# One power instruction for two scales in a macaron block: the order of VectorE's and GpSimd's work in the FFN steps is rewritten

## The reference

```
x = x + 0.5 * ffn(layernorm(x))       # FFN: 128 -> 512 -> 128
x = x + rnn(layernorm(x))             # minGRU, a scan over the 256 tokens of a sequence
x = x + 0.5 * ffn(layernorm(x))       # the same FFN weights again
ffn(v): h = gelu(lin(v, w_up)); return lin(h, w_down)
lin(v, w): v / (rms(v) + 1e-8) @ ternary(w).T,  ternary(w) = sign(w) * (|w| > 0.5 * mean|w|)
layernorm(v): (v - mean) / sqrt(var + 1e-5)
```

## Time and profile before

| what | us |
|---|---|
| median of 3 runs (262.29 to 263.86) | 262.69 |
| the profiled execution's own time | 263.04 |
| its span, first to last instruction | 261.3 |
| mean granted clock of PE, share of full speed | 0.991 |

### The profile page before, as it was taken

How to read it: one execution, slowest core, us unless ns; L and a number is a source line. 1 busy time by engine, 2 the same in 40 slices (tenths; PEclk the granted TensorE clock), 3 DMA queues, 4 the chain that set the end, 5 groups by cost and what they waited for, 6 DMA issues and landing times.

```text
span 261.3 us, 9753 instructions
## 1 busy us (share of the span) xinstructions
PE 236.6 (91%) x3759; PEld 167.1 (64%) x3759; DVE 234.1 (90%) x754; ACT 221.4 (85%) x534; POOL 216.4 (83%) x400
## 2 busy tenths in 40 slices
PE   0759999999998899899999998679999999999992
PEld 0626777777777667655555544357777776777782
DVE  3798799999999998999999999986999999988784
ACT  2377999989998899879999997997899999999861
POOL 5676998989998898599999999998889989997133
PEclk9988999999999999999999999999999999999999
DMA  6990000000000000000000000000111211112114
GB/s 188 300 265 3 4 4 3 3 3 4 3 3 4 3 4 4 3 0 1 3 1 0 0 1 3 3 3 3 43 43 57 67 46 43 43 43 82 46 43 123
DMA packets 18062, 9.73 MB, mean 37 GB/s; under 512 B 608, under 2 KB 17888, under 8 KB 18016
## 3 DMA queue, kind: packets, MB, share of 16 engines
q1 hardware_dynamic: 17744, 8.98, 12.5%
q10 hardware_dynamic: 272, 0.13, 0.2%
HBM read 4.92 MB, written 4.19 MB: 35 GB/s over the span
## 4 chain that ended last, share of the span: by engine, by line
PE 53%; DVE 21%; ACT 7%; POOL 7%; issue 6%; DVEq 0%; ACTq 0%; POOLq 0%
PE Y L502 17%; PE U L458 9%; PE G L489 9%; PE U L459 8%; DVE hidden L701 5%; PE T L439 4%; ACT h_hi L330 4%; DVE st L719 3%; DVE h_lo L654 3%; PE U L518 2%; DVE cand L691 2%; DVE mv L619 2%; PE G L478 2%; POOL xn L236 2%; POOL root L212 2%
## 5 line engine op out<-in xcount | busy, mean ns | idle before, releaser
L654 DVE SCALAR_TENSOR_TENSOR h_lo<-h_hi,U 128x1024 f16<-128x1024 f16 x63 | 75.6, 1215 | 10.0 <-ACT h_hi L330 9.6
L324 ACT ACTIVATE U<-U 128x1024 f32<-128x1024 f32 x63 | 64.7, 1026 | 15.3 <-PE U L459 14.4
L236 POOL TENSOR_SCALAR xn<-X,neg_mean,rstd 128x128 f32<-128x128 f32 x156 | 67.8, 447 | 6.9 <-DVE rstd L624 4.2
L330 ACT ACTIVATE h_hi<-U 128x1024 f16<-128x1024 f32 x63 | 64.7, 1027 | 1.0
L502 PE MATMUL Y<-down_w,h_hi 128*128 128x128 f16 x496 | 59.4, 220 | 0.0
L502 PE MATMUL Y<-down_w_half,h_lo 128*128 128x128 f16 x496 | 59.0, 219 | 0.0
L458 PE MATMUL U<-xt_hi,up_w 128*128 128x512 f16 x128 | 49.2, 384 | 9.4 <-DVE h_lo L654 7.5
L212 POOL TENSOR_TENSOR root<-mv,half 128x8 f32<-128x8 f32 x31 | 51.0, 1644 | 2.3
L459 PE MATMUL U<-xt_lo,up_w 128*128 128x512 f16 x128 | 49.2, 384 | 0.0
L502 PEld LDWEIGHTS Y<-down_w_half,h_lo 128*128 128x128 f16 x496 | 48.5, 98 | 0.4
L502 PEld LDWEIGHTS Y<-down_w,h_hi 128*128 128x128 f16 x496 | 47.7, 98 | 1.6
(11 more groups left out here) (101 smaller groups left out, 415.2 us busy)
## 6 DMA issues: line engine op xcount, KB each, us to landing
X<-in_L_attn_x SPq DMA_DIRECT2D x16, 256.0 KB, 5.3
out_x<-X SPq DMA_DIRECT2D x15, 256.0 KB, 2.8
up_raw<-in_L_ffn_w_up SPq DMA_DIRECT2D x1, 256.0 KB, 4.5
down_raw<-in_L_ffn_w_down SPq DMA_DIRECT2D x1, 256.0 KB, 4.7
out_x<-X SPq DMA_DIRECT2D x1, 128.0 KB, 1.9
out_x<-X ACTq DMA_DIRECT2D x1, 128.0 KB, 2.9
gate_raw<-in_L_attn_Wh SPq DMA_DIRECT2D x1, 64.0 KB, 3.7
gate_raw<-in_L_attn_Wi SPq DMA_DIRECT2D x1, 64.0 KB, 3.6
```

The lines of the kernel that those rows point to most:

```text
L236: m = eng.tensor_scalar(xn[:, n % 2, t, :], X[:, c, :], neg_mean[l][:, c:c + 1], rstd[l][:, c:c + 1], ALU.add, ALU.mult)
L324: eng.activation(U[part][:], U[part][:], ACT.Gelu, scale=1.0 / XN_SPLIT).then_inc(gelu_done, 1)
L330: eng.mul(h_hi[:, F % 2, 2 * part:2 * part + 2, :], U[part][:], H_SPLIT).then_inc(h_hi_done, 1)
L654: vec.scalar_tensor_tensor(out=h_lo[:, F % 2, 2 * part:2 * part + 2, :], in0=h_hi[:, F % 2, 2 * part:2 * part + 2, :], scalar=-1.0 / H_SPL ...
```

## The change

The two powers become one. `ACT` writes the sum of squares of FFN group F into a fourth column of `mv`, beside the variance of the group that is five later in the same layer (`rides_with`, `rider`). POOL then takes one power over 128x4x3 for `ln_roots(l, g)` and adds pairs into a `den` of 128x8, and DVE's `scales` makes both scales in one reciprocal of 128x8. The last five FFN groups of each layer ("alone") keep `rms_step`. The joint power waits for `ssq_done` of F.

Around it the order is rewritten. On POOL `norm` stands first in every step, ahead of the joint power of `ln_roots(k+3)`, and `ln_moments(k+4)` stands last. On DVE in FFN0, `scales(0, k+3)` stands between the two `h_low` of step k, and `stats` and `mean_var` of group k+4 stand behind `add_ffn(k-2)`. The turn into the RNN issues the gates of its first groups one by one on other PSUM banks, and ahead of `gram(15)` and `down(15)`; some RNN steps take five tiles of later statistics instead of four. At the end PE lays `gram(31)` between the tiles of `down(30)`, and the last rows are added and stored in smaller parts.

```
 def ln_roots(l, g):
-    if l == 0 or g >= BY_ACT:
-        ln_moments(l, g)
+    F = rider(l, g)
+    w = 2 if F is None else 3
     pool.wait_ge(var_set[l], 2 * (g if l == 0 else g + 1))
-    eng.tensor_tensor(root[l][:, g % 2], mv[l][:, cols(g), 1:3], half[:], ALU.pow).then_inc(root_done[l], 1)
+    if F is not None:
+        pool.wait_ge(ssq_done, F + 1)
+    eng.tensor_tensor(root[l][:, g % 2, :, 0:w], mv[l][:, cols(g), 1:1 + w], half[:, :, 0:w], ALU.pow).then_inc(root_done[l], 1)
...
 # POOL
-for s in range(0, 3 * groups):
+for s in range(2, 3 * groups):
...
+    if s + 2 < 3 * groups and r != 1:
+        norm(s + 2)
+    if 2 <= k < groups - 3:
+        ln_roots(0, k + 3)
...
+    if 1 <= q < groups - 3:
+        ln_roots(2, q + 3)
...
+    if k + 4 < groups:
+        ln_moments(0, k + 4)
...
+    if 0 <= q < groups - 4:
+        ln_moments(2, q + 4)
...
 # DVE, FFN0
+for k in range(2, groups):
+    if k + 1 < groups:
+        low_part(k + 1)
...
+    h_low(k, 0)
+    if 2 < k < groups - 3:
+        scales(0, k + 3)
+    h_low(k, 1)
...
+    finish_ffn(k - 2)
+    if k + 4 < groups:
+        stats(0, k + 4)
+        mean_var(0, k + 4)
...
+    later_stats(k)
...
 # PE, the end
-gram(2 * groups - 1)
-down(2 * groups - 1)
+down(LAST - 1, [0])
+last_gram(0)
+last_gram(1)
+last_gram(2)
+down(LAST - 1, [1])
+last_gram(3)
+down(LAST - 1, [2, 3])
+down(LAST)
```

More of the change, by code:

```diff
@@ L145, in cols, with rides_with, rider, rstd @@
             return slice(g * TILES, g * TILES + n)
+        def rides_with(F):
+            l, k = (0, F) if F < groups else (2, F - groups)
+            return (l, k + 5) if k + 5 < groups else None
+        def rider(l, g):
+            return None if g < 5 else g - 5 if l == 0 else g - 5 + groups
+        alone = [F for F in range(2 * groups) if not rides_with(F)]
+        def rstd(l, c):
+            return rstd1[:, c:c + 1] if l == 1 else scale[l][:, c, 0:1]
+        def y_factor(F, t):
+            if not rides_with(F):
+                return y_scale[:, F % 4, t:t + 1]
+            l, g = rides_with(F)
+            return scale[l][:, g * TILES + t, 1:2]
+        def y_ready(engine, F):
+            if rides_with(F):
+                l, g = rides_with(F)
+                engine.wait_ge(rstd_done[l], g + 1)
+            else:
+                engine.wait_ge(y_scale_done, alone.index(F) + 1)
         def by_both(n):
@@ L281, in _ @@
             pool.wait_ge(scaled_done, 1)
-            eng.tensor_tensor(X[:, cols(groups - 2), :], X[:, cols(groups - 2), :], scaled, ALU.add).then_inc(pool_added, 1)
+            eng.tensor_tensor(X[:, tiles - 8:tiles - 6, :], X[:, tiles - 8:tiles - 6, :], scaled[:, 0:2, :], ALU.add).then_inc(pool_added, 1)
         @block.scalar
@@ L368, in sum_squares @@
                 act.wait_ge(gram_done, F + 1)
-                if F >= 2:
-                    act.wait_ge(rms_ready, F - 1)
+                if not rides_with(F) and alone.index(F) >= 2:
+                    act.wait_ge(rms_ready, alone.index(F) - 1)
                 for t in range(TILES):
-                    m = eng.activation(square_junk[:, F % 2, t, 0:HALF], G[:, t, 0:HALF], ACT.Relu, accum_out=ssq[:, F % 2, t:t + 1])
+                    if rides_with(F):
+                        l, g = rides_with(F)
+                        m = eng.activation(square_junk[:, F % 2, t, 0:HALF], G[:, t, 0:HALF], ACT.Relu, scale=4.0 / dff,
+                                           accum_out=mv[l][:, g * TILES + t, 3:4])
+                    else:
+                        m = eng.activation(square_junk[:, F % 2, t, 0:HALF], G[:, t, 0:HALF], ACT.Relu,
+                                           accum_out=ssq[:, F % 2, t:t + 1])
                 m.then_inc(ssq_done, 1)
@@ L395, in _ @@
                 ffn(k, k + 1)
-                if k >= 11:
+                if 11 <= k < groups - 1:
                     rnn_moments(k - 11)
             act.preload_act_table(ACT.Sigmoid)
-            for r in range(groups):
+            gate(0, 0)
+            turned(groups + 1)
+            gate(0, 1)
+            norm_tile(groups + 2, 2)
+            norm_tile(groups + 2, 3)
+            gate(0, 2)
+            gate(1, 0)
+            turned(groups + 2)
+            rnn_moments(4)
+            norm_tile(groups + 3, 2)
+            gate(1, 1)
+            norm_tile(groups + 3, 3)
+            gate(1, 2)
+            sum_squares(groups - 1)
+            rnn_moments(5)
+            for r in range(2, groups):
                 turned(groups + r + 1)
@@ L479, in gram @@
                               start=True, stop=False, tile_position=(0, n * HALF))
[L480 to L490, removed]
@@ L491, in gram, with products @@
-                m.then_inc(gram_done, 1)
+            def products(F, t, c, last):
+                for right in (h_hi, h_lo):
+                    for n in range(2):
+                        e = slice(t * P + n * HALF, t * P + (n + 1) * HALF)
+                        m = pe.matmul(gram_of(F)[n * HALF:(n + 1) * HALF, t, 0:HALF], h_hi[:, F % 2, c, e], right[:, F % 2, c, e],
+                                      start=False, stop=last and right is h_lo, tile_position=(0, n * HALF))
+                return m
@@ L493, in down, with last_gram @@
+            def last_gram(c):
+                pe.wait_ge(h_lo_done, 2 * LAST + max(c, 1))
+                if c == 0:
+                    mask(LAST)
+                for t in range(TILES):
+                    m = products(LAST, t, c, t == TILES - 1 and c == chunks - 1)
+                if c == chunks - 1:
+                    m.then_inc(gram_done, 1)
             def down(F, rows=range(TILES)):
@@ L512, in gates @@
                     pe.wait_ge(scan_done, g - 1)
[L513 to L518, removed]
+                pe.matmul(z(g)[n], gate_w[:, n, :], xt[:, g % 2, :], start=True, stop=True).then_inc(gate_ready, 1)
             def turn_back(g):
@@ L556, in _ @@
                 down(k - 1)
-            for r in range(groups):
-                turn(groups + r + 1)
[L559 to L564, removed]
+            turn(groups + 1)
+            for n in range(3):
+                gate(0, n)
+            gate(1, 0)
+            turn(groups + 2)
+            gate(1, 1)
+            gate(1, 2)
+            gram(groups - 1)
+            down(groups - 1)
+            turn_back(0)
+            for r in range(2, groups):
+                turn(groups + r + 1)
+                for n in range(3):
+                    gate(r, n)
+                turn_back(r - 1)
             up(groups, 0)
@@ L685, in add_ffn, with add_scaled_rows @@
                     m.then_inc(ffn_added, 1)
+            def add_scaled_rows():
+                dve.wait_ge(scaled_done, 1)
+                vec.tensor_tensor(X[:, tiles - 6:tiles - 4, :], scaled[:, 2:4, :], X[:, tiles - 6:tiles - 4, :],
+                                  ALU.add).then_inc(rows_added, 1)
             def candidate(g):
@@ L746, in _ @@
             weight_limits(1)
+            stats(0, 3)
+            mean_var(0, 3)
+            low_part(1)
+            scales(0, 2)
+            h_low(0, 0)
             ternary_below(1)
+            h_low(0, 1)
             ternary(1)
             halve_down()
-            for k in range(2):
-                low_part(k + 1)
-                if k == 0:
-                    scales(0, 2)
+            scales(0, 3)
+            low_part(2)
+            h_low(1, 0)
+            stats(0, 4)
+            mean_var(0, 4)
@@ L754, in _ @@
+            h_low(1, 1)
+            stats(0, 5)
+            mean_var(0, 5)
+            for k in range(2, groups):
+                if k + 1 < groups:
+                    low_part(k + 1)
+                if k == 2:
+                    scales(0, 4)
                 h_low(k, 0)
-                if k == 1:
-                    scales(0, 3)
-                stats(0, k + 3)
-                mean_var(0, k + 3)
+                if 2 < k < groups - 3:
+                    scales(0, k + 3)
                 h_low(k, 1)
-            for s in range(2, 3 * groups + 2):
-                k, r, q = s, s - groups, s - 2 * groups
-                F = k if k < groups else groups + q
-                in_ffn = 0 <= k < groups or 0 <= q < groups
-                if k + 3 < groups:
-                    stats(0, k + 3)
-                    mean_var(0, k + 3)
-                if k + 2 < groups:
-                    scales(0, k + 2)
-                if s > 2 * groups and 0 <= s - 29 < groups:
-                    scales(2, s - 29)
+                if k == 2:
+                    scales(0, 5)
+                if diagonal_by_max(k - 1):
+                    sum_squares(k - 1)
+                finish_ffn(k - 2)
+                if k + 4 < groups:
+                    stats(0, k + 4)
+                    mean_var(0, k + 4)
+                if k == groups - 1:
+                    candidate(0)
+                later_stats(k)
@@ L771, in _ @@
+            scan(0)
+            candidate(1)
+            finish_ffn(groups - 2)
```

(61 more changed lines are left out.)

204 lines of the change are left out of this document (130 added, 74 removed).

## The result

The changed kernel takes 287.81 us in the median (286.93 to 288.39), the kernel before, timed beside it, 262.62. The ratio is 1.0948 with a 95% interval of 1.0909 to 1.0986. The forecast was 290.0, range 282 to 297. The profiled execution's own time is 287.73 us, its span 285.6.

The account below looks back on a forecast made before the run. No engine stood out at 83% to 91% busy; POOL's work equalled a step, 5.54 us. Terms 29.2 + 1.1 - 1.6 - 0.5 - 0.5 - 0.4 = +27.3 on 263.04 gave 290.3, forecast as 290.0 us, range 282 to 297.

Parts of the forecast that it names:

- The loop: FFN0, steps 3 to 12: DVE's reciprocal, statistics, POOL's moments, tiles, joint power and `den` form a closed chain; +29.2 us.
- Its price: One turn through DVE and POOL in FFN0: DVE 3.55, POOL 4.93, handovers 0.13, together 8.61 us per step.
- The power: POOL's joint power of 128x12: taken as 2.35 us, with bounds 1.72 and 2.81.
- the ten steps: FFN0 from `add_ffn(0)` to `add_ffn(10)`: 86.1 us against 56.9 before, +29.2 us.
- The last steps of FFN0: From `add_ffn(10)` to the last `h_low`: some 14.2 us of DVE's own work against 15.8 before, -1.6 us.
- The turn and the RNN: From FFN0 into the RNN: first gates no longer wait for the last `h_low`; -0.5 us, bounds 0 and -1.5.
- FFN2: FFN2 steps: gain bounded by PE's 0.5 us of pauses in eight steps; -0.5 us, bounds 0 and -1.5.
- PE's clock: PE in FFN0: parts of each step may run at 1.2 GHz, 7 us of work in 8.6; costed at nothing.
- the head's trace: At the kernel's start, before the change: after a 2.80 us pause PE's granted clock was 0.50, then 0.98 after 3.2 us unbroken work.
- The second rival: PE at 1.2 GHz throughout FFN0's ten steps: they cost 23 us more, 313 us in all; chance 4%.
- The range: Whole kernel: 282 to 297 us, holding 90%, from the joint power's bounds and small terms of -2.5 to +1.5.

## Why the prediction was right

- *The loop* was the step that decided, and it was right in its place, its members and its sign: the waits forecast for DVE (over 3 us, 3.14 measured), POOL (about 3.5, 3.64) and PE (about 3, 2.88) are there, PE's at this length only in about every other step. Opening it by two lines takes 27 us off, and each part that leaves it shortens the step by its own length, to within 0.12 us.
- *Its price* was 8.61 and measured 8.36. The power was right (2.35). POOL's moments and tiles were mis-sized: 0.56 and 1.82 were read in the order of before, moments behind tiles and the power behind the moments; in the new order they take 0.46 and 1.71. Why is open, since the tiles and the power behind them wait for semaphores in the new order too. That is 2.1 of the 2.5 us by which the ten steps were overestimated.
- *The last steps of FFN0* gave 0.8 instead of 1.6: I summed DVE's own work, but two `h_low` still wait for ACT (0.36 and 0.56 in the rows at 125.33 and 130.66).
- *The turn and the RNN* together gave nothing. The five-tile steps lie in the RNN, not in the turn where I counted them, and cost there what the turn gained: from scan 2 to scan 15 the RNN takes 48.4 us instead of 47.2, and from the last `h_low` to scan 2 the turn takes 14.4 instead of 15.4.
- *FFN2* gained more than I allowed. I took PE's pauses, 0.5 us in eight steps, as a bound, but the eight steps fell from 44.30 to 43.20 with PE busy 42.99 (209.70 to 252.90 in the windows view below). The same matmuls count fewer busy us when the step is shorter, so PE's busy time is no floor. Their rows overlap (a product of `down` lasts 0.22 us and the next starts 0.06 after it), which may be why; no run shows it.

```profile
209.70:252.90 43.20, 42.99 (x879) 32.76 (x878) 41.74 (x128) 41.01 (x105) 37.61 (x67) 1.00 0.18 52
```

- *PE's clock* fell as the head's trace suggested, in four of the ten steps, and cost nothing, as forecast. In those steps the granted clock is 0.80 over the whole step and PE is busy 6.9 us (7 forecast); in the others it is 1.00 and some 5.5. The four falls follow pauses of 2.7 to 2.9 us, and a low step leaves a pause of only some 1.4, behind which the clock stays up; but it also stayed up behind one pause of 2.88, at 40.59. The second rival needed the clock low throughout. A restart after each pause, as the prediction quotes the rule, does not give that, so the prediction's step from the rule to this rival's value was wrong.
- *The range* was rounded inwards at its lower end and outwards at its upper: its own terms, 283.7 - 2.5 and 294.6 + 1.5, give 281.2 to 296.1.

## What to carry to other kernels

When instructions of two in-order queues change places, follow every pair of waits round: what a queue waits for, what stands behind that wait, and who waits for that. If the path closes on itself within one step, no step can be shorter than its length, however idle the engines look in sum. FFN2 has such a path too, forecast at 5.2 us, under its step, and it costs nothing there. Here the source of the chain, the statistics, had to move ahead by some 4 us of DVE's work, to the beginning of its step. An instruction that is merged inherits the latest input and the earliest consumer of both.

## What the hardware showed that I had not expected

- A power on GpSimd costs 0.70, 1.01, 1.65 and 2.28 us for 2, 4, 8 and 12 values a partition: nearly 0.16 us for each value and 0.37 to 0.39 besides. Merging two powers saves that second part and the gap, no more.
- Small instructions on GpSimd that last 0.20 us start sometimes 0.28 us apart and sometimes 0.17: moments to power 0.28 in the earlier trace rows, moments to tiles 0.17 in the timeline after. A wait for the result of the one ahead does not explain it, since the two moments stand 0.28 apart as well and the second waits for nothing in the order rows. The cause is open; in the loop the shorter distances were worth 0.2 us a turn.
